# A fused retention and Hadamard-FFN block in float32: scores of four heads by full-height matmuls, and by two 64-row halves of the array

## The reference, cut to what matters

```python
h = layernorm(x) * (1 + ca) + sa                 # x: 4 batches x 512 tokens x 256
q, k = rope(h @ Wq.T), rope(h @ Wk.T)            # 4 heads of 32
v = h @ Wv.T                                     # 4 heads of 64
# retention over chunks with a state S, decay gamma**distance:
attn = einsum('bhid,bhjd->bhij', q, k) * dmask   # the scores, causal
o = einsum('bhij,bhjv->bhiv', attn, v) + (q @ S) * g_in
o = o * rsqrt(mean(o * o) + eps) * gnorm_w
x = x + ga * ((o * silu(h @ Wg.T)) @ Wo.T)
h = layernorm(x) * (1 + cb) + sb
x = x + gb * (fwht(silu(h @ W1.T) * (h @ W3.T)) @ W2.T)
```

## Time and profile before

| | us |
|---|---|
| median of 3 runs (286.5 to 286.86) | 286.54 |
| the profiled execution | 287.58 |
| its span, first to last instruction | 285.4 |
| TensorE busy with matmuls, 1888 of them | 258.5 (91%) |
| TensorE's weight loads | 240.7 (84%) |
| VectorE busy | 173.6 (61%) |
| GpSimd busy | 138.1 (48%) |
| ScalarE busy | 122.0 (43%) |

### The profile page before, as it was taken

The page is one execution under the profiler, slowest core; times in us unless marked ns, Lnnn a source line. Parts: engine busy times, 40 slices in busy tenths (PEclk is TensorE's granted clock), DMA queues, the critical chain, the costliest instruction groups (busy, mean ns, idle before and its releaser), DMA issues.

```text
span 285.4 us, 5010 instructions
## 1 busy us (share of the span) xinstructions
PE 258.5 (91%) x1888; PEld 240.7 (84%) x1888; DVE 173.6 (61%) x340; ACT 122.0 (43%) x249; POOL 138.1 (48%) x159
## 2 busy tenths in 40 slices
PE   1696797789999999999999999999998999899992
PEld 1564585679889989999999998999998999799992
DVE  2317777899696675747476786658458555572210
ACT  2414545476247324723473146623454344233320
POOL 2066226415745491474728383755166627542632
PEclk9999689999999999999999999999999999999998
DMA  6997300100010002000200002000100011001011
GB/s 191 383 379 271 147 2 1 37 3 0 2 37 1 2 0 57 20 2 1 75 1 2 0 0 76 0 3 0 40 32 5 2 37 39 0 0 39 5 34 37
DMA packets 11294, 14.02 MB, mean 49 GB/s; under 512 B 1156, under 2 KB 9220, under 8 KB 11016
## 3 DMA queue, kind: packets, MB, share of 16 engines
q1 hardware_dynamic: 11272, 13.71, 14.5%
HBM read 9.77 MB, written 2.11 MB: 42 GB/s over the span
## 4 chain that ended last, share of the span: by engine, by line
PE 68%; DVE 11%; POOL 8%; issue 4%; DMA 4%; ACT 2%; SPq 2%; POOLq 0%; DVEq 0%; ACTq 0%
PE pu L298 25%; PE pacc L298 13%; PE pd L298 5%; PE pa L298 4%; PE pb L298 4%; DMA wmod_sb<-wmod 3%; PE pc L305 3%; DVE xn L622 2%; PE pc L298 2%; POOL rso L784 2%; PE pacc L348 2%; POOL qk L809 1%; POOL hid_lo L830 1%; PE pstate L298 1%; PE pstate L323 1%
## 5 line engine op out<-in xcount | busy, mean ns | idle before, releaser
L298 PE MATMUL pu<-h_hi,w_hi 128*128 128x256 f32 x256 | 73.1, 286 | 0.0
L298 PE MATMUL pu<-h_hi,w_lo 128*128 128x256 f32 x256 | 72.4, 283 | 0.0
L298 PE MATMUL pu<-h_lo,w_hi 128*128 128x256 f32 x256 | 72.4, 283 | 0.0
L830 POOL TENSOR_TENSOR hid_lo<-hid,hid_hi 128x512 fp32r<-128x512 f32 x32 | 43.1, 1350 | 34.9 <-ACT hid_hi L772 34.8
L298 PEld LDWEIGHTS pu<-h_hi,w_hi 128*128 128x128 f32 x256 | 49.0, 191 | 0.4
L298 PEld LDWEIGHTS pu<-h_lo,w_hi 128*128 128x128 f32 x256 | 49.0, 191 | 0.3
L298 PEld LDWEIGHTS pu<-h_hi,w_lo 128*128 128x128 f32 x256 | 49.0, 191 | 0.0
L298 PE MATMUL pacc<-w_hi,hid_hi 128*128 128x256 f32 x128 | 37.6, 294 | 0.7 <-POOL hid_lo L830 0.7
L298 PE MATMUL pacc<-w_lo,hid_hi 128*128 128x256 f32 x128 | 36.2, 282 | 0.0
L298 PE MATMUL pacc<-w_hi,hid_lo 128*128 128x256 f32 x128 | 36.1, 282 | 0.0
L767 ACT ACTIVATE silu<-pu 128x512 f32<-128x512 f32 x32 | 19.0, 594 | 31.6 <-PE pu L298 31.2
(11 more groups left out here) (136 smaller groups left out, 620.3 us busy)
## 6 DMA issues: line engine op xcount, KB each, us to landing
raw<-w SPq DMA_DIRECT2D x4, 512.0 KB, 9.9
out<-xres SPq DMA_DIRECT2D x8, 256.0 KB, 2.4
qb<-qkt SPq DMA_DIRECT2D x28, 64.0 KB, 2.0
xres<-x SPq DMA_DIRECT2D x1, 1536.0 KB, 13.9
wmod_sb<-wmod SPq DMA_DIRECT2D x1, 1024.0 KB, 8.1
raw_w<-w SPq DMA_DIRECT2D x1, 1024.0 KB, 10.0
gates<-gate_dram SPq DMA_DIRECT2D x1, 1024.0 KB
xres<-x SPq DMA_DIRECT2D x2, 256.0 KB, 4.3
```

Source lines behind the costliest of these rows:

```text
L298: mm = pe.matmul(ps, a, c, start=start and n == 0, stop=stop and n == len(ops) - 1, skip_group_check=True)
L830: pool.tensor_tensor(hid_lo[:, k % 2], hid32[:, k % 2], hid_hi[:, k % 2].bitcast(F32), ALU.subtract).then_inc(p_hid.sem, 1)
```

## The change

The scores of both tiles of a unit become one step. Each matmul covers two heads: 64 rows of weights (partitions 0 to 63 or 64 to 127 of k) and 256 columns, a block-diagonal of two heads, so qb has half its columns. Group g = 0 (heads 0, 1) writes bank pc, g = 1 (heads 2, 3) bank pd, and tile j the columns 256j to 256j+255 of both. That makes 2 tiles x 3 products x 2 groups = 12 matmuls of 256 columns for six of 512. The list keeps both entries on TensorE, but the second does nothing. The two banks become one tensor, pheads, and VectorE's mask for a tile reads half of both banks. The semaphore t_s counts once a unit, and every o waits for the second mask.

```diff
-        qkt, qb = sb("qkt", [P, 2, 2, 2, 2, P], F32R), sb("qb", [P, 2, 2, HEADS, P], F32R)
+        qkt, qb = sb("qkt", [P, 2, 2, 2, 2, P], F32R), sb("qb", [P, 2, 2, 2, P], F32R)
...
-        pa, pb, pc, pd, pstate = (bank(n) for n in "pa pb pc pd pstate".split())
+        pa, pb, pstate = (bank(n) for n in "pa pb pstate".split())
+        pheads = ctx.enter_context(nc.psum_tensor("pheads", [P, 2, 512], F32))
+        pc, pd = pheads[:, 0], pheads[:, 1]
...
-                    sp.wait_ge(t_s.sem, t_s.after(u - 1, 1))
+                    sp.wait_ge(t_s.sem, t_s.after(u - 1))
                     sp.wait_ge(d_qklo.sem, d_qklo.after(u))
                     for h in range(HEADS):
                         rows = slice(h * DK, (h + 1) * DK)
-                        sp.dma_start(qb[rows, :, :, h, :].rearrange("p e t i -> p (e t) i").bitcast(F32),
+                        sp.dma_start(qb[rows, :, :, h % 2, :].rearrange("p e t i -> p (e t) i").bitcast(F32),
...
-                elif kind == "sc":
-                    if u == 0 and k == 0:
+                elif kind == "sc" and k == 0:
+                    if u == 0:
                         pe.wait_ge(a_qb0.sem, 1)
                         pe.wait_ge(d_qb0.sem, 1)
-                    elif k == 0:
+                    else:
                         pe.wait_ge(s_qb.sem, s_qb.per * u)
-                    if u and k == 0:
                         pe.wait_ge(a_h2x.sem, a_h2x.after(u - 1))
-                    elif u:
                         pe.wait_ge(d_br.sem, d_br.after(u - 1))
-                    three(pz[k][:, :], [((qkt[:, par, 0, k, 1], qkt[:, par, 1, k, 1]),
-                                         (qb[:, 0, k], qb[:, 1, k]))]).then_inc(t_s.sem, 1)
+                    for j in range(2):
+                        for n, (a, c) in enumerate(((0, 0), (0, 1), (1, 0))):
+                            for g in range(2):
+                                rows = slice(g * 2 * DK, (g + 1) * 2 * DK)
+                                mm = pe.matmul(pz[g][:, j * 2 * P:(j + 1) * 2 * P], qkt[rows, par, a, j, 1],
+                                               qb[rows, c, j].rearrange("p h i -> p (h i)"), start=(n == 0),
+                                               stop=(n == 2), skip_group_check=True)
+                    mm.then_inc(t_s.sem, 1)
...
                 elif kind == "o":
                     out_k = pz[k][:, :].rearrange("p (h s v) -> p h s v", h=HEADS, s=2)
+                    pe.wait_ge(d_p.sem, d_p.after(u, 1))
                     if t:
-                        pe.wait_ge(d_p.sem, d_p.after(u, k))
                         pe.wait_ge(p_s.sem, states(u, k))
...
-                    dve.wait_ge(t_s.sem, t_s.after(u, k))
-                    dve.tensor_tensor(p32[:, k], pz[k][:, :].rearrange("p (h i) -> p h i", h=HEADS),
-                                      causal.unsqueeze(1).to_broadcast([P, HEADS, P]), ALU.mult
+                    dve.wait_ge(t_s.sem, t_s.after(u))
+                    dve.tensor_tensor(p32[:, k].rearrange("p (g h) i -> p g h i", g=2),
+                                      pheads[:, :, k * 2 * P:(k + 1) * 2 * P].rearrange("p g (h i) -> p g h i", h=2),
+                                      causal.unsqueeze(1).unsqueeze(1).to_broadcast([P, 2, 2, P]), ALU.mult
                                       ).then_inc(d_p.sem, 1)
```

More of the change, by code:

```diff
@@ L213, in adaln_block_kernel @@
             sem(n) for n in "t_qk d_rope p_rope t_qkt a_qkt d_qklo a_k p_k".split())
-        t_vg, a_vg, d_vlo, t_s, d_p, a_p, d_plo, t_o, a_o, d_o, a_sq, p_y0, d_ss, p_vo, p_rso, d_y = (
-            sem(n, 2) for n in "t_vg a_vg d_vlo t_s d_p a_p d_plo t_o a_o d_o a_sq p_y0 d_ss p_vo p_rso d_y".split())
-        t_kv, d_s, a_s, p_s = (sem(n) for n in "t_kv d_s a_s p_s".split())
+        t_vg, a_vg, d_vlo, d_p, a_p, d_plo, t_o, a_o, d_o, a_sq, p_y0, d_ss, p_vo, p_rso, d_y = (
+            sem(n, 2) for n in "t_vg a_vg d_vlo d_p a_p d_plo t_o a_o d_o a_sq p_y0 d_ss p_vo p_rso d_y".split())
+        t_s, t_kv, d_s, a_s, p_s = (sem(n) for n in "t_s t_kv d_s a_s p_s".split())
         t_yt, a_yt, d_yt, t_wo, d_br, d_x1, d_st2, d_mv2, p_ve2, p_rs2, d_xn2 = (
@@ L564, in step @@
                         rows = slice(h * DK, (h + 1) * DK)
-                        ins = dve.tensor_copy(qb[rows, 1, :, h, :], qkt[rows, par, 1, :, 0].bitcast(F32))
+                        ins = dve.tensor_copy(qb[rows, 1, :, h % 2, :], qkt[rows, par, 1, :, 0].bitcast(F32))
                     ins.then_inc(d_qb0.sem, 1)
@@ L714, in step @@
                         rows = slice(h * DK, (h + 1) * DK)
-                        ins = act.activation(qb[rows, 0, :, h, :], qkt[rows, par, 0, :, 0].bitcast(F32),
+                        ins = act.activation(qb[rows, 0, :, h % 2, :], qkt[rows, par, 0, :, 0].bitcast(F32),
                                              ACT.Copy)
```

## The result

The changed kernel takes **289.17 us** (median of 6 runs, 287.91 to 289.93) against 286.7 for the kernel before on the same chip (286.5 to 287.15): ratio 1.0079, 95% interval 1.0053 to 1.0105. It is 2.5 us slower where 286.4, 0.1 faster, was forecast; a second measurement gave 289.64 and 1.0088. (One execution can stand a microsecond off its median: the profiled ones took 289.93 after and 287.58 before.)

What follows compares the result with a forecast made beforehand. TensorE's own stream was taken as the bound (busy 91% of the span). Terms -1.15 + 0.08 + 0.84 + 0.15 = -0.08 us, set against the 286.54 median, gave 286.4 us; range 284.2 to 290.4.

Steps and rivals of the forecast that it cites:

- the six slots: Score step on TensorE: twelve half-height matmuls run in side-by-side pairs, six slots of 0.12, 0.72 us.
- the changes of shape: Around each score step: switching TensorE into the halves costs 0.07 us and back 0.36, together 0.43.
- Unit 3's wait: Unit 3's first o also waits for the second mask on VectorE and starts later: +0.84 us.
- The mask on two banks: VectorE's masked product keeps 512 columns though its source lies in two banks: still 0.69 us.
- The tests named beforehand: Signs for the profile after: step 1.15 us, new wait before unit 3's o about 0.8, mask still 0.69.
- loads in turn: Rival, score step: weight loads go one after the other at 0.112, step 1.77 us, kernel 290.7 us; chance 23%.
- Unit 0 is off the chain ...; its scores have no term.: Unit 0: the chain runs over VectorE's splits and xn, so its scores add nothing to the sum.
- so nothing is charged: Units 2 and 4: next unit's transposes start 0.45 us later, but h is wanted much later; no cost.
- at no cost: Each unit's four DMAs still carry 64 KB each in 512-byte pieces, 2.0 us to landing; no term.
- way in and six slots, 0.79: Time from the scores' start to VectorE's first p; in unit 6 0.79 us replaces 0.71, +0.08.
- neither gains nor loses: Unit 3's VectorE queue between the two p's: first p at 0.79 instead of 0.90 us changes nothing.
- five units at -0.23: Units 1, 2, 4, 5 and 7: score step 1.15 us for 1.38, together -1.15 us.

Runs made afterwards that it cites:

- experiment 4: Kernel before, with the second tile's scores (still full-height) moved ahead of the next unit's transposes in units 2 and 4: 287.7 us, ratio 1.0026.
- experiments 6: Changed kernel, transposes back ahead of the scores in units 2 and 4, VectorE's second mask right behind the first in units 0, 3, 7: 286.92 us, 1.0002.
- 7: Kernel before (full-height scores) with the same five moves in the TensorE and VectorE lists as experiments 6: 286.74 us, ratio 0.9999.
- experiment 11: Changed kernel with the five list moves of experiments 6 and 36 extra transposes at unit 0, results overwritten: 286.69 us, ratio 0.9991.
- 12: Kernel before with the five list moves of experiments 6 and 30 extra transposes at unit 0, results overwritten: 286.64 us, ratio 1.0002.

## Why the prediction was wrong

**Right.** The pairs run side by side, loads too: 1.10 for 1.15, of which the six slots took 0.72 as forecast and the changes of shape 0.38 for 0.43, half of it on each way (0.07 and 0.36 were forecast). The Trainium skill, "TensorEngine Tiling (Array Packing)", Key Properties, has both sides of this: tiles load and multiply in parallel, and the change of mode drains TensorE. The trace agrees with both; what the changes cost here is 0.38. Unit 3's wait cost 0.92 of lateness for 0.84. In unit 7 the scores begin 2.82 later than before and o 2.61; with the step's 0.28 saved it would have been 2.54, so the mask costs 0.07 for 0.15. Unit 2 is covered. The mask on two banks costs 0.68 for 0.69. The tests named beforehand (step, new wait, mask) all came out for the forecast's own mechanism, and the time still went the other way. That 289.17 lies inside the stated range of 284.2 to 290.4 speaks for nothing: the range reached so far up for loads in turn, which did not happen.

**Wrong, the step that decides: "Unit 0 is off the chain ...; its scores have no term."** That spoke of the scores. But *every* o got the second mask's wait, and of unit 0's o nothing was looked up: the earlier trace rows has units 2, 3 and 7. The row that was missing, o at 37.65 behind a mask that ends at 37.62, would have read "covered by 0.03 us in a stretch at half clock". Alone on the kernel before, this wait costs 1.1 us by the medians (0.4 to 1.6 by the interval) and makes TensorE stand 1.3 in the trace; its mend in the changed kernel gives back 1.1 to 1.3. In the changed kernel's own traces the same stretch ran at half clock and the wait does not show, so how much of the lost time there is the wait and how much the clock stays open.

**Wrong, a smaller one: "so nothing is charged"** for the transposes that slide behind the scores. h was followed to the next unit's qk, where it isn't late; but ScalarE has it ahead of this unit's p_hi, and the first o waits for that. Unit 4 lost its saving (0.13 later instead of 0.28 earlier, 0.41), as the moved transposes alone show on the kernel before (0.47 in the trace).

**Wrong: "at no cost" for the DMAs.** Their number, size and place are as said. One issue on the path took 1.73 us for 0.60, worth 1.1 us in the traces, because the longer instruction stream brought a transfer of the instruction queue beside it. Nothing in the earlier trace rows could tell it.

**Mis-sized, a smaller one: "way in and six slots, 0.79".** In unit 3 the first p starts 1.02 behind the start of the scores (116.96 to 117.98), and TensorE is what it waits for; before it was 0.90. So the queue on VectorE became 0.12 later, where the forecast had it "neither gains nor loses", and unit 6 lost 0.18 for 0.08. The sum had left out the wider distance behind the first pair, 0.10, and it set the 0.79 at which the last slot ends against a 0.90 that holds 0.21 more, from the end of the slots (3 x 0.23 = 0.69) to p.

**Mis-sized: five units at -0.23.** 0.28 is the step's saving, and units 2 and 5 show it (-0.34 and, beside the issue, -0.47); unit 1 keeps 0.05 because h_lo wasn't ready, unit 4 nothing, and from unit 7 to the end it is -0.42. Together -1.28 where -1.15 was forecast, from fewer units.

The sum from the trace: start to u1 +1.26, unit 1 -0.05, unit 2 -0.34, unit 3 +0.92, unit 4 +0.13, unit 5 +0.66 (the issue +1.13, the rest -0.47), unit 6 +0.18, unit 7 to the end -0.42: +2.34. Of the +1.26, 0.86 is there before unit 0's qk, which the change doesn't touch; it lies between -0.6 and +0.9 in the traces of the experiments. The traced execution of before is itself 0.9 above the median, and experiment 4, with the same code up to there, reaches unit 1 at 40.91 and not at 41.84; so the table's start-up is no measure, and it is the runs with and without unit 0's wait that carry its size. As an estimate from the parts, the steps left out come to 1.1 to 1.3 (unit 0), 0.41 (the transposes) and 1.1 (the issue), which is the 2.6 us between the forecast -0.08 and the measured +2.5, or a little more. How much of the start-up's swing belongs to the halves stays open: with equal mends (experiments 6 and 7, 11 and 12) they still did not show their 1 us in the medians, though in experiment 11 no issue was long.

## What to carry to other kernels

When a change gives many places a new wait, look up every one of them, the start-up too, and note how large the cover is and at which clock it was measured: a cover of 0.03 us at half clock is none. A tile that is moved on one engine must be followed through the next engine's list to everything that stands behind it there, and not only to its own reader. A saving of 0.3 us a unit can be real in the trace and is lost in the runs as soon as one DMA issue or the clock of the start-up falls otherwise.

## What the runs showed of the hardware that was not expected

- The two 64-row halves overlap even where three matmuls of one half stand before three of the other: two start at a time, and it is 0.91 us for the twelve in both orders. Going from 128 to 64 rows and back costs 0.19 on each way.
- A DMA issue on SyncE of 0.60 us takes 0.88 to 1.82 where a 16 KB transfer of the instruction queue begins between 0.5 us before and 0.1 after its start, unless it is the first of its row. 96 TensorE instructions more, or 60 to 72 at unit 0, switch this on or off at unit 5, past 165 us.
- TensorE's clock at start-up: behind a stop of 1.3 us (on top of earlier ones) 256-column matmuls came 0.21 apart instead of 0.12 for a while, with a mean granted clock of 0.66 over 5 us. And fourteen traces of kernels that differ little reach unit 1's qk between 39.63 and 43.10 us.
